# Where the low parts of the second part's projection weights are made, in a DeltaNet-and-MLP block with adaptive layer norm on Trainium2

## What is computed

```python
h = layernorm(x) * (1 + ca) + sa
q, k, v = short_conv(h @ Wq), short_conv(h @ Wk), short_conv(h @ Wv)   # 4 taps, silu
beta = sigmoid(h @ Wb); g = -exp(A_log) * softplus(h @ Wa + dt_bias)
...
S = S * exp(g_t); delta = (v_t - k_t S) * beta_t; S = S + k_t delta^T; o_t = q_t S   # 6 heads
...
x = x + ga * ((rmsnorm(o) * norm_weight * silu(h @ Wg)) @ Wo)
x = x + gb * mlp(layernorm(x) * (1 + cb) + sb)     # silu(gate) * up, hidden size 2048
```

## Time and profile before

| | us |
|---|---|
| three runs: lowest, median, highest | 1140.72, 1142.64, 1145.05 |
| the profiled execution | 1141.11 |
| its span, first to last instruction | 1139.3 |
| busy: TensorE / VectorE / ScalarE / GpSimd | 1066.0 / 619.6 / 371.8 / 228.3 |
| busy of TensorE and VectorE within 210 to 230 | 19.04 / 19.48 |
| busy of TensorE and VectorE within 230 to 250 | 15.15 / 19.41 |
| mean granted TensorE clock | 0.971 |

### The profile page before, as it was taken

The page is one execution under the profiler, slowest core; times in us unless marked ns, Lnnn a source line. Parts: engine busy times, 40 slices in busy tenths (PEclk is TensorE's granted clock), DMA queues, the critical chain, the costliest instruction groups (busy, mean ns, idle before and its releaser), DMA issues.

```text
span 1139.3 us, 18747 instructions
## 1 busy us (share of the span) xinstructions
PE 1066.0 (94%) x7396; PEld 863.5 (76%) x7396; DVE 619.6 (54%) x994; ACT 371.8 (33%) x670; POOL 228.3 (20%) x182
## 2 busy tenths in 40 slices
PE   4898989988998999999978999999999999999998
PEld 2685667767776888888756788788888888888886
DVE  3766445998864677776645433333343334325356
ACT  4575465324435333343236112121121211212110
POOL 1322110001014555555331000000000000004092
PEclk8899999999898999999979999999999999999999
DMA  5503326338328455665622101001010000101222
GB/s 192 193 10 102 80 63 166 94 96 200 85 74 196 95 129 126 154 154 126 191 69 65 56 1 38 18 1 56 1 56 1 28 28 1 56 1 65 67 82 110
DMA packets 147350, 94.72 MB, mean 83 GB/s; under 512 B 93376, under 2 KB 124352, under 8 KB 147136
## 3 DMA queue, kind: packets, MB, share of 16 engines
q1 hardware_dynamic: 147264, 93.53, 30.0%
HBM read 62.05 MB, written 31.46 MB: 82 GB/s over the span
## 4 chain that ended last, share of the span: by engine, by line
PE 79%; DVE 9%; ACT 5%; issue 4%; DMA 1%; POOL 1%; SPq 0%; DVEq 0%; ACTq 0%; POOLq 0%
PE ps L1051 75%; ACT t L1351 5%; PE ps L1059 3%; DVE t L1615 3%; DVE t L1707 3%; PE ps L1239 1%; DVE t L1620 1%; DMA t<-in_x 1%; POOL t L2081 1%; DMA t<-scrU 0%; ACT L1373 0%; DVE t L1807 0%; DMA t<-in_wf 0%; DVE t L1625 0%; DVE t L1818 0%
## 5 line engine op out<-in xcount | busy, mean ns | idle before, releaser
L1051 PE MATMUL ps<-t,t 128*128 128x512 f32 (+6 forms) x6528 | 1009.2, 337 | 55.4 <-DMA t<-in_wmod 8.7
L1051 PEld LDWEIGHTS ps<-t,t 128*128 128x128 f32 (+3 forms) x6528 | 803.5, 168 | 237.1 <-issue 43.1
L1615 DVE TENSOR_TENSOR t<-ps,t 128x512 f32<-128x512 f32 (+4 forms) x306 | 209.2, 701 | 255.0 <-PE ps L1051 243.1
L1351 ACT ACTIVATE t<-t 128x512 fp32r<-128x512 f32 (+7 forms) x330 | 185.0, 578 | 340.8 <-DVE t L1615 201.6
L1615 DVE TENSOR_TENSOR t<-t,t 128x512 fp32r<-128x512 f32 (+16 forms) x209 | 161.9, 779 | 116.6 <-ACT t L1351 109.5
L1351 ACT ACTIVATE t<-ps 128x512 f32<-128x512 f32 (+4 forms) x193 | 108.3, 566 | 329.8 <-PE ps L1051 317.0
L2089 POOL TENSOR_TENSOR t<-t,t 128x512 f32<-128x512 f32 x16 | 22.3, 1392 | 404.6 <-DVE t L1615 402.5
L1707 DVE SCALAR_TENSOR_TENSOR t<-ps,t,t 128x511 f32<-128x511 f32 (+2 forms) x108 | 80.4, 747 | 19.8 <-ACT t L1351 17.0
L1059 PE MATMUL ps<-t,t 128*128 128x128 f32 (+1 forms) x388 | 60.9, 292 | 11.9 <-DVE t L1620 8.9
L1351 ACT ACTIVATE t<-ps,t 128x512 f32<-128x512 f32 (+2 forms) x96 | 56.9, 621 | 33.3 <-DVE t L1615 10.7
L1059 PEld LDWEIGHTS ps<-t,t 128*128 128x128 f32 (+1 forms) x388 | 45.8, 149 | 28.0 <-DVE t L1620 12.8
(11 more groups left out here) (51 smaller groups left out, 249.3 us busy)
## 6 DMA issues: line engine op xcount, KB each, us to landing
scrU<-t SPq DMA_DIRECT2D x60, 256.0 KB, 2.6
t<-in_wf SPq DMA_DIRECT2D x16, 768.0 KB, 4.2
t<-scrU SPq DMA_DIRECT2D x32, 288.0 KB, 4.8
t<-in_wmod SPq DMA_DIRECT2D x6, 1024.0 KB, 6.5
t<-scrU SPq DMA_DIRECT2D x32, 192.0 KB, 3.3
t<-in_W SPq DMA_DIRECT2D x19, 256.0 KB, 2.8
t<-in_x SPq DMA_DIRECT2D x16, 256.0 KB, 4.0
t<-in_x SPq DMA_DIRECT2D x32, 128.0 KB, 2.8
```

What stands on the lines that cost most here:

```text
L1051: return e.matmul(o, l, r_, start=start, stop=stop, skip_group_check=True)
L1351: return e.activation(o, i, f, **kw)
L1615: return e.tensor_tensor(o, a, b, op)
```

## The change

For tiles 5 to 18 the subtraction that makes the low part moves from VectorE to GpSimd, at the same step of the plan. It counts in `p_lo` (after the 16 of the activations, so tile j is done at 12 + j), and both waits that stood on `v_wlo`, SyncE's before the load of tile j + 2 and TensorE's before a tile's first projection, follow it through `w_split`. Tiles 0 to 4 stay on VectorE. On GpSimd each operation waits for the one before it (`in_order`).

```diff
@@ -301,7 +301,6 @@
         wh["n"] += 1
         step("split_w", j=j, h=h, free=wh["free"].get(h))
         tick("a_whi")
-        tick("v_wlo")
         if j + 2 < NT1:
             step("load_w", j=j + 2)
         return h
@@ -843,6 +842,9 @@
     def ho(t):
         return t[:, :, :].rearrange("p (a m) t -> p a (m t)", a=2)
 
+    def w_split(j):
+        return (sem("v_wlo"), j + 1) if j < 5 else (sem("p_lo"), 12 + j)
+
     def ff_ready(j):
         return "v_glo", j + 1
 
@@ -897,7 +899,7 @@
 
         def load_w(j):
             if j >= 2:
-                e.wait_ge(sem("v_wlo"), j - 1)
+                e.wait_ge(*w_split(j - 2))
             e.dma_start(Wraw[j % 2][:, :, :], W1[WSEQ[j]]).then_inc(sem(f"d_w{j % 2}"), 16)
 
         for st in plan:
@@ -1098,7 +1100,7 @@
                 h, b = st["h"], st["b"]
                 if st["free"]:
                     e.wait_ge(*at_least(st["free"]))
-                e.wait_ge(sem("v_wlo"), st["wn"])
+                e.wait_ge(*w_split(st["wn"] - 1))
                 for k in range(4):
                     e.wait_ge(sem("p_lo"), 4 * b + k + 1)
                     t = mm3(bank(st["bank"]), WH[h][:, k, :], WL[h][:, k, :], Hhi[:, b, k, :], Hlo[:, b, k, :],
@@ -1677,7 +1679,7 @@
                 ts(gnat[:, n, :], gnat[:, n, :], 0.25, None, ALU.max, None).then_inc(sem("v_gn"), 1)
                 e.wait_ge(sem("v_gn"), k + 4)
                 tt(gnat[:, n, :], gnat[:, n, :], sgn[:, :], ALU.mult).then_inc(sem("v_gn"), 1)
-            elif kind == "split_w":
+            elif kind == "split_w" and st["j"] < 5:
                 j, h = st["j"], st["h"]
                 if st["free"]:
                     e.wait_ge(*at_least(st["free"]))
@@ -1991,6 +1993,13 @@
                 e.wait_ge(sem("a_hi"), 4 * b + k + 1)
                 in_order()
                 signal(e.tensor_tensor(Hlo[:, b, k, :], HF[k][:, :], Hhi[:, b, k, :].bitcast(f32), ALU.subtract), "p_lo")
+            elif kind == "split_w" and st["j"] >= 5:
+                j, h = st["j"], st["h"]
+                e.wait_ge(*at_least(st["free"]))
+                e.wait_ge(sem("a_whi"), j + 1)
+                in_order()
+                signal(e.tensor_tensor(WL[h][:, :, :], Wraw[j % 2][:, :, :], WH[h][:, :, :].bitcast(f32),
+                                       ALU.subtract), "p_lo")
             elif kind == "inv_gm":
                 u = st["u"]
                 if u == 0:
```

## The result

| | before | changed |
|---|---|---|
| median of the runs (lowest to highest), us | 1142.64 (1140.72 to 1145.05), 7 runs | 1150.18 (1147.82 to 1154.72), 7 runs |
| the profiled execution, us | 1141.11 | 1151.71 |
| its span | 1139.3 | 1149.9 |
| busy: TensorE / VectorE / GpSimd | 1066.0 / 619.6 / 228.3 | 1066.0 / 616.1 / 246.4 |

The ratio is 1.0057, with a 95% interval of 1.004 to 1.0074. Times a before of 1142.6 that is +6.5 us (4.6 to 8.5); the two medians alone are 7.5 us apart, which lies within that. The forecast was +5.5, 1147.9, within a range of 1142.3 to 1151.5.

What follows compares the result with a forecast made beforehand. VectorE's inverse plus SyncE's queue behind it was taken to set the time. Inverse -0.7, queue +5.3, decays +1.1, rest -0.2, clock 0 gave +5.5 us; counted from the mean 1142.4, 1147.9, range 1142.3 to 1151.5.

Steps and rivals of the forecast that it cites:

- The queue: SyncE's load of tile 18, waiting for GpSimd's memset and tile 16's subtraction, holds the DMAs returning the inverse: +5.3 us.
- The collisions: In the inverse, GpSimd's subtractions of tiles 11, 13, 15 hold VectorE's two-operand steps 1.0 us each, +3.0; under taps nothing.
- The subtractions' worth: Six subtractions leave VectorE's inverse, 0.61 us each from start to start: -3.7 us.
- the inverse: VectorE's inverse in all, six subtractions gone less three held steps: -0.7 us, bounds -3.7 and +3.2.
- The decays: Before TensorE's decay sums, GpSimd's decay operands, behind tile 6's subtraction, run beside VectorE's two-operand steps: +1.1 us.
- The rest: Tiles 5 to 9, 17 and 18 free VectorE time, mostly without effect: -0.2 us, between -0.6 and 0.
- VectorE's busy time: Sign of the forecast: VectorE's busy time falls by 14 x 0.68 = 9.6 us.
- The clock: TensorE's half clock after the longer stall at the merge costs the same as now: 0, between -1 and +2 us.
- A: Rival: engines don't hold each other up in inverse or decays, the queue costs 5.3: +1.4 us, 1143.8; chance 0.22.
- B: Rival: in SyncE's queue the DMAs returning the inverse aren't held: -3.9 us, 1138.5; chance 0.05.
- C: Rival: GpSimd costs VectorE more in decays and under taps, and the half clock lasts longer: +9.5 us, 1151.9; chance 0.23.

Runs made afterwards that it cites:

- return_first: The change with all fourteen subtractions on GpSimd, but SyncE's load of tile 18 planned behind the DMAs that bring the inverse back; ratio to the kernel before 0.9996.
- only_sixteen: The kernel before with tile 16's subtraction alone on GpSimd; ratio to the kernel before 1.0035.
- odd_three: The kernel before with the subtractions of tiles 11, 13 and 15 alone on GpSimd; ratio to the kernel before 0.9999, inverse 75.68 us.
- odd_twice: The kernel before with the subtractions of tiles 11, 13 and 15 alone on GpSimd, each issued twice in a row; one run, 1148.12 us, inverse 78.63.
- even_three: The kernel before with the subtractions of tiles 10, 12 and 14 alone on GpSimd; ratio to the kernel before 0.9979, inverse 73.28 us.
- sixteen_back: The change with tile 16's subtraction alone back on VectorE; ratio to the kernel before 1.0007.
- load_behind: The kernel before with only SyncE's load of tile 18 planned behind the DMAs that bring the inverse back; ratio to the kernel before 0.9993.
- held_and_behind: The kernel before with tiles 10 to 15 on GpSimd, 11, 13, 15 held until the taps, tile 18's load behind the returning DMAs; ratio 0.9961.
- held_odd: The kernel before with tiles 10 to 15 on GpSimd, 11, 13 and 15 held back until the taps; ratio to the kernel before 0.9973.
- clear_three: The kernel before with a GpSimd memset released where the subtractions of tiles 11, 13 and 15 were, no subtraction moved; one run, 1144.95 us.

## Why the prediction was right

**The queue** (+5.3): 5.04 measured, on exactly the forecast chain: 2.67 + 0.16 + 1.26 + 0.03 to the load, then 0.92 for the load and the store, forecast at 0.41 + 0.82 = 1.23; that is the difference. `return_first` and `only_sixteen` show it from both sides. Not in the forecast was that the DMAs then took 6.44 to the transposes instead of 6.09, so that the way from the inverse's end to the merge grew by 5.4.

**The collisions** (+3.0 for three, 1.0 each): `odd_three` gives 1.08 + 3 x 0.60 = 2.9, `odd_twice` 2.95 more for three more. Right in place, number and size. Under taps I took nothing: `even_three` lost 3 x 0.48 - 1.32 = 0.1 in all. The prediction's reading that GpSimd had been idle from 100 to 268 us was wrong: it had `inv_gm` and memsets between 122 and 176. Within the inverse it was idle, so the sum doesn't suffer.

**The subtractions' worth** (-3.7) was mis-sized. The step "6 x 0.61" took the distance to the next start as the gain; three of the six stood between two dependent steps and were worth 0.48. So -3.2, and the inverse came out at -0.18 in place of -0.7.

**The decays** (+1.1): 1.29, near it partly by luck, since two terms that I had left out nearly cancel. The pair of 96 elements and the one of 4x512 stretched (+0.66, +0.52), the one at 120.11 did not (0.26 for 0.25), and the cast between, which I had left out, did: 0.82 for 0.21, so +0.61. Against them, tile 6's subtraction no longer stood among these steps (118.68 in before), which took off 0.5: 1.19 + 0.61 - 0.5 = 1.3. The Trainium skill has the cast among VectorE's instructions that can take the shared ports ("SBUF — State Buffer", Who interferes with whom); the rows agree, and I had read only its line on two SBUF inputs.

**The rest** (-0.2): no run measured it by itself, and the table shows nothing of it. Put together, the pieces give -0.2 + 5.4 + 1.3 = +6.5, a microsecond above the forecast; the inverse, the queue and the decays each came out higher than forecast, the inverse by most (0.5).

**VectorE's busy time** was to fall by 9.6 and fell by 3.5. That was a slip within my own reasoning: a held instruction counts as busy, so the three collisions (about 3.0) and the decays' stretches (1.8, and 0.6 in the copies behind them) had to be taken off, 5.4 of the 6.1 missing. A fall by less than the work removed is the sign of collisions.

**The clock** (0): stretches of the changed kernel, with the columns of the earlier trace rows:

```profile
295.00:297.00 2.00, 2.00 (x6) 1.56 (x5) 1.55 (x4) 0.00 (x0) 0.00 (x0) 0.50 0.92 144
297.00:299.00 2.00, 1.80 (x51) 1.17 (x50) 0.15 (x1) 0.42 (x2) 0.00 (x0) 0.84 1.13 270
```

It came back some 7 us after TensorE resumed at 290.32; before it was some 6 after 281.19 (1.00 in 288 to 290). TensorE's 84 small matmuls behind the first merge took 6.83 us instead of 6.25. That is no price of the longer stall: behind the short stalls of `sixteen_back` and `return_first` they took 7.05 and 7.14, and over all the profiles 5.77 to 7.14. A cost of the longer stall can't be seen, and the 0 stands within its bounds.

**The rivals.** A (collisions cost nothing) falls with `odd_three`, B (the return is not held) with the 5.04 us. C is not what happened in the sum, though the profiled execution came near its +9.5 for another reason, below.

**What stays open.** The profiled execution of the change has 10.6 us, of which the pieces above explain 6.5: -0.18 in the inverse, 5.04 held, 0.35 for the slower landing (6.44 - 6.09), 1.29 at the decays. Of the rest, 1.0 lies ahead of the change and 1.6 in the clock at 103. That makes the 9.1 by which TensorE is late at the merge (290.32 against 281.19). At the start of the third part it stood still once more, before and after:

```profile
375.42 5.26 PE L1051 MATMUL ps<-t,t 128*128 128x512 f32 x42 [1.48 <-issue]
```

```profile
383.87 7.94 PE L1053 MATMUL ps<-t,t 128*128 128x512 f32 x42 [4.28 <-POOL t L2078]
```

It starts these 42 matmuls 8.45 us late and ends them 11.13 late, because they took 2.7 us longer: the granted clock was 0.50 in 383 to 389, where it had been 1.00 in 375 to 381 of the kernel before. The same stop for GpSimd, of 2.2 to 2.6 us, stands in the profiles of `only_sixteen`, `even_three`, `load_behind` and `held_and_behind`, and not in the other eight (1.3 to 1.5 us). `load_behind` has no subtraction moved, and `held_and_behind` is one of the two fastest, so it comes without the moved subtractions and is not what made the change slow. Nor does the landing of the load of Wo sort the runs: 8.8 us after the change and 6.5 before, but 8.1 and 8.3 in `sixteen_back` and `held_odd` without the stop, and 7.2 and 6.8 in `load_behind` and `held_and_behind` with it. The cause stays open; no run tested it.

## What to carry to other kernels

Before an operation is moved to an idle engine, follow who waits for it, in each queue, and what stands ahead of it on the new engine: here a load nobody was in a hurry for carried GpSimd's wait into SyncE's queue and in front of the one transfer that TensorE stood still for. On VectorE and GpSimd, put a GpSimd instruction that reads SBUF under VectorE's operations on PSUM; here a pair of semaphore waits at three tiles did so and turned a gain of 0.2 us in the inverse into 3.2. Price what is taken out by the start of the next instruction with and without it, since dependent neighbours give part of it back.

## What the runs showed of the hardware

- A GpSimd subtraction of 512 elements (1.28 us) among two-operand steps held one of them by 0.96 to 1.0 us on average (`odd_three`, `odd_twice`; single rows 0.95 to 1.09); a GpSimd memset of 1.38 us held none (`clear_three`).
- GpSimd was held too, when it started beside a two-operand step of VectorE that was already running: 1.54 and 1.40 us for tiles 12 and 14 instead of 1.28.
- A cast of 96 elements, one SBUF input, went from 0.21 to 0.82 us beside GpSimd's multiplications.
- A load of 256 KB and a store just ahead of the 16 DMAs of 96 KB made the first ones land about 1.0 us later (6.09 against 4.99 to 5.17 with the load behind them and the store 0.3 us sooner). I had thought of the load as an issue of 0.41 only.
